# Statistics of the last layer norm taken behind the attention's row additions, and half of the feed-forward network's first weights split inside the norm's block

## The reference, cut to what matters

```python
x = res + _cross_attention(h, xf_2, wq2, bq2, wk2, bk2, wv2, bv2, wo2, bo2, bias_k2, bias_v2)
h = _layer_norm(x, ln_mlp_scale, ln_mlp_offset)
h = jax.nn.gelu(h @ w_fc1 + b_fc1, approximate=False) @ w_fc2 + b_fc2
return x + h

def _layer_norm(x, scale, offset):
    mu = jnp.mean(x, axis=-1, keepdims=True)
    var = jnp.var(x, axis=-1, keepdims=True)
    return (x - mu) * jax.lax.rsqrt(var + LN_EPS) * scale + offset
```

## Time and profile before

| what | value |
|---|---|
| time, median of 3 runs | 2740.22 us |
| lowest and highest run | 2735.76, 2745.87 us |
| the profiled execution's own time | 2739.51 us |
| span from its first to its last instruction | 2737.7 us |
| TensorE matmul busy, instructions | 2478.0 us (91%), 13944 |
| weight loads busy | 2167.3 us (79%) |
| VectorE busy | 1394.6 us (51%) |
| ScalarE busy | 1139.6 us (42%) |
| GpSimd busy | 1122.3 us (41%) |
| TensorE's mean granted clock | 0.95 |

### The profile page before, as it was taken

How to read it: one execution, slowest core, us unless ns; L and a number is a source line. 1 busy time by engine, 2 the same in 40 slices (tenths; PEclk the granted TensorE clock), 3 DMA queues, 4 the chain that set the end, 5 groups by cost and what they waited for, 6 DMA issues and landing times. The chain is left out here.

```text
span 2737.7 us, 37676 instructions
## 1 busy us (share of the span) xinstructions
PE 2478.0 (91%) x13944; PEld 2167.3 (79%) x13944; DVE 1394.6 (51%) x2335; ACT 1139.6 (42%) x2439; POOL 1122.3 (41%) x498
## 2 busy tenths in 40 slices
PE   7888679989998888899889999989997999999698
PEld 5666334479895555699889999979996999999698
DVE  4566541278885431243346666533334666665633
ACT  3677111232233211223366666622235666665321
POOL 1100322251222110452287978826215887976300
PEclk9999869999998889999999999999999999999799
DMA  7453611589993015244744544315285444442300
GB/s 227 122 122 78 213 63 48 154 245 237 235 227 125 8 54 174 90 157 165 250 152 163 161 146 156 127 53 206 103 272 178 155 138 155 145 159 85 109 29 25
DMA packets 218058, 390.93 MB, mean 143 GB/s; under 512 B 88900, under 2 KB 127836, under 8 KB 217108
## 3 DMA queue, kind: packets, MB, share of 16 engines
q1 hardware_dynamic: 217876, 388.52, 45.8%
HBM read 291.70 MB, written 104.92 MB: 145 GB/s over the span
## 5 line engine op out<-in xcount | busy, mean ns | idle before, releaser
L1851 PE MATMUL att_ring<-ca_pp,att_arena 128*128 128x400 f32 (+1 forms) x2304 | 437.5, 348 | 26.5 <-POOL att_arena L1933 14.8
L1851 PEld LDWEIGHTS att_ring<-ca_pp,att_arena 128*128 128x128 f32 (+1 forms) x2304 | 422.0, 191 | 36.0 <-POOL att_arena L1933 20.2
L1922 POOL TENSOR_TENSOR att_arena<-att_arena 128x1448 fp32r<-128x1448 f32 x64 | 212.1, 3314 | 253.6 <-ACT att_arena L1939 253.6
L1851 PE MATMUL att_ring<-att_arena,qk_wh 128*128 128x362 f32 x1024 | 255.6, 331 | 0.0
L2535 DVE TENSOR_TENSOR ca_yl<-att_ring,att_arena 128x400 fp32r<-128x400 f32 x256 | 146.6, 573 | 203.8 <-ACT att_arena L2494 203.8
L1933 POOL TENSOR_TENSOR att_arena<-state_X,att_arena 128x1536 fp32r<-128x1536 f32 x64 | 224.4, 3506 | 5.0
L1930 POOL TENSOR_TENSOR att_arena<-state_X,att_nothing 128x1536 fp32r<-128x1536 f32 x64 | 176.0, 2750 | 47.7 <-DMA state_X<-in_ctx 47.7
L1851 PE MATMUL att_ring<-att_arena,qk_wl 128*128 128x362 f32 x512 | 172.9, 338 | 18.6 <-POOL att_arena L2116 18.2
L1851 PEld LDWEIGHTS att_ring<-att_arena,qk_wh 128*128 128x128 f32 x1024 | 185.2, 192 | 0.0
L2494 ACT ACTIVATE att_arena<-att_ring 128x400 fp32r<-128x400 f32 x256 | 128.9, 503 | 92.9 <-PE att_ring L1851 92.6
L1945 ACT ACTIVATE att_kstage<-att_score,att_shift 100x362 f32<-100x362 f32 x256 | 143.8, 563 | 44.6 <-DVE att_shift L1958 44.6
(11 more groups left out here) (404 smaller groups left out, 6010.3 us busy)
## 6 DMA issues: line engine op xcount, KB each, us to landing
att_arena<-keys SPq DMA_DIRECT2D x64, 724.0 KB, 5.1
state_X<-in_ctx SPq DMA_DIRECT2D x64, 512.0 KB, 3.9
queries<-att_arena SPq DMA_DIRECT2D x16, 1600.0 KB
att_arena<-queries SPq DMA_DIRECT2D x64, 400.0 KB, 3.9
keys<-rec_stage SPq DMA_DIRECT2D x32, 724.0 KB, 4.5
keys<-att_kstage SPq DMA_DIRECT2D x32, 724.0 KB, 3.2
l_arena<-kept_value SPq DMA_DIRECT2D x176, 100.0 KB, 5.4
state_X<-in_ctx SPq DMA_DIRECT2D x64, 210.0 KB, 4.2
```

What stands on the lines that cost most here:

```text
L1851: issued = nc.tensor.matmul(out, x, y, start=(first and k == 0), stop=(last and k == count - 1))
L1922: self.nc.gpsimd.tensor_tensor(self.kl[:, n % 2].bitcast(F32R), self.kl[:, n % 2], self.kh[:, n % 2].bitcast(F32), ALU.subtract).then_inc( ...
```

## The change

It does two things. `attention` gets a tile `stats`, for the second attention block alone, and `add_rows` takes a batch's BN_STATS right after its add, waiting for that add; the norm is called with `ready`, so `row_statistics` begins with the aggregates. The tile is allocated in `program`, ahead of everything else but X, `ident` and `columns`.

The first 2 MB copy of w_fc1 becomes two of 1 MB, columns 0 to 511 (semaphore `first_in`) and 512 to 1023. `layer_norm_transposed` is given four `pieces`, each a 128 x 512 chunk of the first: ScalarE copies one behind each of the batches 4 to 7, VectorE subtracts all four behind its last batch. In the network's block the first piece of the first part is left out on both, the counts are one lower, and TensorE's first four units wait for no weights. `wh` and `wl` are allocated before the norm.

```diff
@@ layer_norm_transposed
+            piece_high = pieces and sc.sem("piece_high")
...
                         nc.scalar.activation(write_out(b)[0], affine[:, b % 2], ACT.Copy).then_inc(high_done, 1)
+                    if pieces and b >= B - len(pieces):
+                        if b == B - len(pieces):
+                            act.wait_ge(arrived, 16)
+                        nc.scalar.activation(pieces[b - B][0], pieces[b - B][2], ACT.Copy).then_inc(piece_high, 1)
...
+                for i, (high, low, raw) in enumerate(pieces):
+                    dve.wait_ge(piece_high, i + 1)
+                    nc.vector.tensor_tensor(low, raw, high.bitcast(F32), ALU.subtract)
@@ attention, add_rows
                 nc.vector.tensor_tensor(X[:, b, :], X[:, b, :], bank_of("rows", half, i)[0:L, :], ALU.add).then_inc(rows_added, 1)
+                if stats:
+                    dve.wait_ge(rows_added, b + 1)
+                    nc.vector.bn_stats(stats[:, b, :], X[:, b, :])
@@ mlp
-        start_copies(nc, raw_in[0], loads(0)[0:1])
+        first_in = sc.sem("first_in")
+        wh = [sc.sb(f"wh{i}", [P, CC * FH], F32R) for i in range(2)]
+        wl = [sc.sb(f"wl{i}", [P, CC * FH], F32R) for i in range(2)]
+        by_column = [t[:].rearrange("p (c n) -> p c n", c=CC) for t in (wh[0], wl[0], raw[0])]
+        start_copies(nc, first_in, [(by_column[2][:, :, 0:FH // 2], fc1[:, :, 0:FH // 2])])
+        start_copies(nc, raw_in[0], [(by_column[2][:, :, FH // 2:FH], fc1[:, :, FH // 2:FH])])
         start_copies(nc, raw_in[1], loads(0)[1:2])
         start_copies(nc, small_in, [(bias[:], a["fc1_columns"]), (row[:], a["fc2_rows"])])
         layer_norm_transposed(nc, "lnm", X, 1e-5, column("L3_xattn_ln_mlp_scale"), column("L3_xattn_ln_mlp_offset"),
-                              ident, lambda b: (highT[:, b], lowT[:, b]), "split")
+                              ident, lambda b: (highT[:, b], lowT[:, b]), "split", stats,
+                              [[t[:, c, 0:FH // 2] for t in by_column] for c in range(CC)], first_in)
@@ mlp, sync
-                    sp.wait_ge(weight_ready, PIECES * (2 * (part - 1) + m + 1))
+                    sp.wait_ge(weight_ready, PIECES * (2 * (part - 1) + m + 1) - 1)
@@ mlp, high on ScalarE, and the same in low on VectorE
+                for i, (dst, src) in enumerate(zip(pieces(wh[m][:], m), pieces(raw[m][:], m))):
+                    if part == m == i == 0:
+                        continue
@@ mlp, TensorE
-                        pe.wait_ge(weight_ready, PIECES * 2 * part + f // FP + 1)
+                        if n >= FP:
+                            pe.wait_ge(weight_ready, PIECES * 2 * part + f // FP)
...
-                pe.wait_ge(weight_ready, PIECES * (2 * part + 2))
+                pe.wait_ge(weight_ready, PIECES * (2 * part + 2) - 1)
@@ program
+        stats = sc.sb("stats", [L, B, 6])
```

More of the change, by code:

```diff
@@ L100, in add_and_sum, with layer_norm_transposed @@
     return store
-def layer_norm_transposed(nc, prefix, X, eps, weight, offset, ident, write_out, out_engines, ready=None):
+def layer_norm_transposed(nc, prefix, X, eps, weight, offset, ident, write_out, out_engines, ready=None, pieces=(), arrived=None):
     with Scope(nc, prefix + "s") as outer:
@@ L2340, in _, with attention @@
                     t.scores(pe, 1)
-def attention(nc, prefix, t, X, weights, scratch):
+def attention(nc, prefix, t, X, weights, scratch, stats):
     HALVES = STEPS // BH
@@ L2645, in _, with mlp @@
             turn_rows(1)
-def mlp(nc, a, X, ident, column, out, output_gone):
+def mlp(nc, a, X, ident, column, out, output_gone, stats):
     FH = F3 // 2
@@ L2671, in mlp @@
         layer_norm_transposed(nc, "lnm", X, 1e-5, column("L3_xattn_ln_mlp_scale"), column("L3_xattn_ln_mlp_offset"),
-                              ident, lambda b: (highT[:, b], lowT[:, b]), "split")
-        wh = [sc.sb(f"wh{i}", [P, CC * FH], F32R) for i in range(2)]
-        wl = [sc.sb(f"wl{i}", [P, CC * FH], F32R) for i in range(2)]
+                              ident, lambda b: (highT[:, b], lowT[:, b]), "split", stats,
+                              [[t[:, c, 0:FH // 2] for t in by_column] for c in range(CC)], first_in)
         act32 = sc.sb("act32", [P, 2, HALF])
@@ L2720, in high @@
                     act.wait_ge((full, out_full)[m], (HIDDEN, OUTS)[m] * part)
-                for dst, src in zip(pieces(wh[m][:], m), pieces(raw[m][:], m)):
+                for i, (dst, src) in enumerate(zip(pieces(wh[m][:], m), pieces(raw[m][:], m))):
+                    if part == m == i == 0:
+                        continue
                     nc.scalar.activation(dst, src, ACT.Copy).then_inc(high_w, 1)
@@ L2743, in low @@
                 for i, (dst, src, rounded) in enumerate(zip(pieces(wl[m][:], m), pieces(raw[m][:], m), pieces(wh[m][:], m))):
-                    dve.wait_ge(high_w, PIECES * (2 * part + m) + i + 1)
+                    if part == m == i == 0:
+                        continue
+                    dve.wait_ge(high_w, PIECES * (2 * part + m) + i)
                     nc.vector.tensor_tensor(dst, src, rounded.bitcast(F32), ALU.subtract).then_inc(weight_ready, 1)
@@ L2825, in _, with attention_block @@
             turn_rows(1)
-def attention_block(nc, a, X, spare, ident, column, i):
+def attention_block(nc, a, X, spare, ident, column, i, stats=None):
     weights = [a[f"L3_xattn_w{w}{i}"] for w in "qkvo"]
@@ L2837, in attention_block @@
                     column(f"L3_xattn_ln{i}_scale"), column(f"L3_xattn_ln{i}_offset"), FILLED_GROUPS)
-        attention(nc, f"ca{i}", t, X, weights, scratch)
+        attention(nc, f"ca{i}", t, X, weights, scratch, stats)
 def program(nc, a, out):
@@ L2863, in program @@
         clear_semaphores(nc)
-        attention_block(nc, a, X, spare, ident, column, 2)
+        attention_block(nc, a, X, spare, ident, column, 2, stats)
         clear_semaphores(nc)
-        mlp(nc, a, X, ident, column, out, output_gone)
+        mlp(nc, a, X, ident, column, out, output_gone, stats)
         Scope.retired.append(output_gone)
```

## The result

| | before | after |
|---|---|---|
| time, median of 22 runs each | 2740.96 us | 2752.28 us |
| lowest and highest run | 2735.76, 2752.14 us | 2738.6, 2769.84 us |
| the profiled execution's own time | 2739.51 us | 2739.94 us |
| span | 2737.7 us | 2738.2 us |
| VectorE busy | 1394.6 us | 1401.4 us |

The ratio is 1.0041, 95% interval [1.0027, 1.0055]: 11 us slower. That is under the 0.5% called "no change", but above the range of 2736 to 2749. The profiled execution is one of the fastest of the 22, so it shows the stretch that the change works in, and not where the median's 11 us come from.

The account below looks back on a forecast made before the run. TensorE bounds the network, so only when its first matmul runs counts. +5.9 - 1.3 + 1.8 - 4.5 = +1.9 us on 2739.51 gave 2741.4 (2742.1 on the median 2740.22), called "no change"; range 2736 to 2749.

Parts of the forecast that it names:

- Part 1, the adds: Second attention's row adds: each add must land before its BN_STATS, so the new section starts 5.9 us later.
- Part 1, T to N: From the new section's start (T) to the first normalisation (N): 5.38 us instead of 6.67, -1.3, held by sync engine's issues.
- A: Rival: the sync engine doesn't hold the barrier before the first normalisation; that stretch 2.30 us, sum -1.2; 20 in 100.
- B: Rival: the copy queue counts packets, so the stretch before the first normalisation takes 8.2 us, sum +4.7; 12 in 100.
- Part 2: Norm's end: eight small instructions splitting weights, four ScalarE copies and four VectorE subtractions, lengthen the norm by 1.8 us.
- three subtractions are hidden: Norm's end: VectorE's first three weight subtractions cost nothing; only the last, 0.68 us at its best, adds time.
- N to E: From first normalisation to the norm's last instruction (before: GpSimd's last low half): 14.9 us against 13.13, +1.8.
- Part 3: Network's opening: TensorE's first four units wait for no weights, so 0.5 us instead of 5.03 before its first matmul, -4.5.
- Rival C: Network's first matmuls: TensorE's clock returns sooner after a shorter pause, saving 2.9 us, sum -1.0; 5 in 100.
- The sum: All three parts, from the attention's last row adds to the network's first matmul: +1.9 us.
- Rival D: All layers: the statistics' tile moves later tiles 192 bytes; 1 ns on each of 13944 matmuls, +13.9 us; 3 in 100.
- The range: Whole kernel: 2736 to 2749 us, including up to +0.9 for VectorE subtractions slowed beside GpSimd's low halves.

Follow-up runs that it names:

- e6: The whole change with statistics in unread entries of `columns` (no tile moves) and the two small copies issued ahead of the 4 MB of weights: 2739.62 us, ratio 1.0004.
- e5: The whole change, but with the statistics in entries of `columns` that nothing reads any more, so no tile moves: 2739.48 us, ratio 1.0012 to the kernel before.
- e2: The kernel before with only an unused tile of 192 bytes where the change has its statistics: 2744.01 us, ratio 1.0022.
- e16: The kernel before with only an unused tile of 192 bytes where the change has its statistics, run a second time: 2750.18 us, ratio 1.0029.
- e10: The change plus 64 unused bytes behind its statistics' tile, so later tiles move by 256 bytes: 2742.18 us, ratio 1.0012 to the kernel before.
- e1: The change run again, unedited: 2746.35 us, ratio 1.0026 to the kernel before.
- e17: The kernel before, attention tiles behind the arena moved 192 bytes, GpSimd waiting for each low half of value and output weights: 2739.71 us, 1.0009 (1.0105 without the wait).

## Why the prediction was right or wrong

- **Part 1, the adds.** Right: +5.7 for +5.9, statistics 0.70 to 0.73 us behind each add.
- **Part 1, T to N.** Right in kind: the reciprocal is done 1.75 us after T, and VectorE then waits 3.91 us for the barrier. The sync engine's issues took 5.11 us for the 4.83 assumed, so -1.0 for -1.3. The bias stalled for 2.11 instead of 3.11, but the three weight copies took 2.06 instead of 0.94 for two: the sum hardly moves. Rivals A and B are both refuted (5.67 us from T to N, not 2.30 or 8.2), and e6 shows the hold directly.
- **Part 2.** The term of the sum mis-sized most: "three subtractions are hidden". VectorE came to its first at 2579.82, when ScalarE had made two of the high halves, and did all four in 4.15 us, beside two GpSimd low halves of 1.50 and 1.14 instead of 1.03. ScalarE's last copy was done 14.06 us after N (2582.13), as forecast (14.2), but VectorE wasn't free for the last subtraction. N to E rose by 2.8 and not 1.8. Part of the range named this contention, +0.9. The rule of the Trainium skill ("SBUF — State Buffer", "Who interferes with whom"), that the two lock each other out for whole instructions, stood nearer, with its +2.4. The trace agrees: GpSimd's two at their usual 1.03 are 2.06 us of the 4.15, and 2.1 are left for the four subtractions, 0.52 each.
- **Part 3.** Right, -4.7 for -4.5; the network runs at 37.85 and 34.99 us per 192 matmuls as before. Rival C is refuted.
- **The sum** was +1.9 and is +2.8. It agrees with e5, 1.0012 [0.9998, 1.0027].
- **Rival D is the step that failed.** It had the place right, the 192 bytes, and gave them 3 in 100, because it priced one mechanism alone, a nanosecond on each of 13944 matmuls, and "no row speaks for it". In the sum itself the moved addresses stood at nothing. The runs put them at 1.0022 (e2) and 1.0029 (e16), 5.8 and 9.6 us at the medians, and without them the change falls back to 1.0012 (e5, e10); that is what took the time out of the range. The matmuls did not slow: those of 128x400 in the last layer took 343 ns at the median before and after, and 344 in e2. What the shift did was to make another engine's instruction 54 ns longer, and in three kernels with tiles moved VectorE missed its turn at such an instruction, 5.8 to 6.9 us a time. That this is what e2 and the change lose is argued from these, and not shown. Rows that would have warned were in the profile before: the instruction for the softmax's shift has 0.16 us of work and a median of 2.08, up to 4.44, and 52 of the 64 began within a GpSimd instruction (the other 12 took 0.16 to 0.17). I had read only the 28 us that the edit touches.
- **The range** took the scatter of three runs, 10 us, for the kernel's. The 22 executions of the change lie between 2738.6 and 2769.84, those of the kernel before between 2735.76 and 2752.14. Up to three lost turns would make this spread, and one or two the median's 8 us; that is an estimate from 5.8 to 6.9 us each, and none was caught in a profile of the change.

Open: why 192 bytes, and not 64, 128 or 256, lengthen GpSimd's low half; why a low half of 4.67 us loses turns that one of 4.62 doesn't; how much of the change's own 11 us (e1: 8) are lost turns; and what makes the first three layers take up to 12 us more in one execution than in another.

## What to carry to other kernels

Where a short VectorE instruction waits in the shadow of long GpSimd ones, look at what follows at GpSimd's end: back-to-back instructions can pass it over, and in e17 one semaphore wait between them gave it its turn for 0.08 us. A new tile is an edit to every tile behind it, so compare it with an unused tile of the same size before its effect is put down to the work. And issue small copies ahead of megabytes where the issuing engine takes part in the next barrier: here 2.9 us in the profile (e6).

## What the runs showed that I had not expected

- A 128x2048 GpSimd subtraction takes 4.62 us, or 4.67 with its tiles 192 bytes further on, with the same work.
- Where it took 4.67, VectorE's waiting instruction was sometimes (6 of 44 times) passed over by two further GpSimd instructions, ending 8.9 to 9.0 us after its start instead of about 3.
- The sync engine's five issues took 5.11 us with 4 MB in front and 2.3 with the small copies first.
